# A state-space layer and attention in one kernel: a scan's end in seven PSUM banks, both norms from one formula, and the step size's chain inside the query and key products

## The chip, the cores and the metric

The kernel runs on one core of one Trainium2 chip. The metric is the time of one execution on the device in microseconds (us). The profile is that of one further execution. Engines: TensorE (PE; PEld is its weight load), VectorE (DVE), ScalarE (ACT), GpSimd (POOL) and SyncE (SP), which issues nearly all DMAs.

## What is computed

A gated block with two layers over four sequences of 512 rows of 512 values (`x`) and a context of 256 values per row. The first layer is a Mamba layer on the context, gated by the normed rows; the second is attention with rotary positions and a mixture of experts. Cut from the reference, with the names of the kernel's batches `s` (first layer) and `b` (second):

```python
x = einsum('ed,bld->bel', in_proj_w, hidden_states)          # in-projection
u = silu(conv(x, conv_w, 4 taps) + conv_b)
x_dbl = einsum('ke,bel->bkl', x_proj_w, u)                   # dt_lo, B, C
delta = softplus(einsum('er,brl->bel', dt_proj_w, dt_lo) + dt_proj_b)
def step(state, xs):
    d_t, B_t, C_t, u_t = xs
    dA = exp(d_t[..., None] * A)
    state = state * dA + (d_t * u_t)[..., None] * B_t[:, None, :]
    return (state, einsum('bn,ben->be', C_t, state))
y = (scan(step) + D * u) * silu(z)                           # z: the layer-normed rows of x
```

The attention that follows norms the new rows twice: a layer norm, (x - m) / sqrt(v + 1e-5), and on its result an RMS norm with 1e-6 under the root. Then come queries, keys (both rotated), values, a causal softmax in 16 heads of 32, an output product, another RMS norm, a router with top 2 of 8 experts, and a shared expert.

## The kernel before

**Rounds.** `round_(b, s)` runs for b from -1 to 3 with s = b + 1: the attention of batch b beside the Mamba scan of batch s. I call a round by its b. Each engine has its own program, with the same order of rounds; semaphores tie them. A round has a projection stage and then 16 units (`units(b, s)`, 64 scans of 128x512, 16 quads of heads). Round -1 has no attention (s = 0 alone), and round 3 no scan (`last_units`). After it comes the expert stage (`moe_stage`), which the change doesn't touch.

**A scan's end.** A scan (L1616, VectorE) of step k needs its decay (`decay`, L1174, ScalarE, exp into a PSUM bank) and its input (`driven`, L2095, GpSimd, `DU` times a row of B in one of four slots of `GB`). TensorE turns four states at a time (`turn_states`, L652) and VectorE adds them, weighted, to `YA` (`add_state`, L1626). For s > 0 all states go through one bank, `HT0`, so that each group waits for the addition before; for s = 0 two banks take turns. After the last addition TensorE turns the gate z (`turn_z`, L663, 16 transposes, two banks), VectorE multiplies (`scan_out`, L1633) and adds the result to the rows in `xa` (x1, L1637).

**The projection stage.** VectorE takes the statistics of x1; GpSimd makes both norms' factors in ten operations on 128x4 (`norms`, L2112 to L2121), each behind the one before; ScalarE scales the rows (`rows`, L1188), TensorE turns them, ScalarE and VectorE split them in a high and a low part (`h1_round`, `h1_rest`), TensorE makes the values. Between these lie the next batch's in-projection (L602), its convolution (ScalarE `conv_start`, VectorE `conv`) and what is left of the batch before: `finish(b - 1, 3, step)`, the last 128 rows' output product, norm and router.

**The products.** The loop over m from 0 to 7 then makes four query and four key products (`product`, 12 matmuls each), ScalarE adds a bias (`bias`, L1201), TensorE rotates (`rotate`, L696), GpSimd multiplies by the cosine (`rope_cos`, L2127) and VectorE by the sine and adds (`rope_out`, L1658 and L1662). Beside these, for m from 2 to 5, one quarter each of the step size delta: product (`delta`, L642), absolute value on ScalarE, relu on VectorE. Its softplus ends behind the loop: exp for m = 6, then Ln (`delta_log`, another table of ScalarE), and on VectorE four times `delta_sum` (L1598) and `delta_u` (L1604). The first `driven` waits for all four sums, because `GB` and the softplus' tile `TS` are one piece of memory.

The eight PSUM banks are `A[0]` to `A[3]` (together `SB`, named scores in traces), bank4 (`CX`, `WK`), bank5 (`PB`), and bank6 and bank7 (`HT0`, `HT1`). The lines that set the scan's end:

```python
def state_bank(s, q):
    return (HT0, A[0])[q % 2] if s == 0 else HT0
def decay_bank(s, k):
    return (HT1, A[1])[k % 2] if s == 0 else HT1
```

## Time and profile before

| | us |
|---|---|
| median of 3 runs | 1853.08 |
| lowest and highest | 1849.81, 1853.17 |
| the profiled execution, whole | 1852.96 |
| its span, first to last instruction | 1851.2 |
| busy: PE, DVE, ACT, POOL | 1504.1, 1180.0, 892.6, 806.3 |
| mean granted clock of TensorE, share of full speed | 0.878 |

The profiled execution is 0.1 us from the median, so that its timeline can be read against the median without a correction; 1.8 us of it lie outside the span. TensorE has the largest share (81%), but a sum over the span says little, since its stages have different limits. Round 0 begins at about 187 us, round 1 at 436, round 2 at 690 and round 3 at 945, each with its projection stage (90 to 95 us with a scan to follow); the expert stage fills the time from about 1165 us on. TensorE's clock has two levels, 1.2 and 2.4 GHz; 1.00 in a row is the upper one, 0.50 the lower.

### The profile page before, as it was taken

The page shows a single profiled execution, that of the slowest core. Times are in us where ns is not written, and L with a number is a line of the kernel's source. Part 1 is how long each engine was busy: PE and PEld are TensorE (multiplying, and loading weights), DVE is VectorE, ACT ScalarE, POOL GpSimd, SP SyncE. Part 2 cuts the span into 40 slices and gives each one's busy share as a digit, 9 for nine tenths or more (in the row PEclk, how much of TensorE's full clock was granted, in tenths as well). Part 3 has the DMA queues.
Part 4 walks back from the last instruction along what each step waited for, and adds up shares of the span by engine and source line. Part 5 has one row for each costly group of instructions (what it writes and reads, how often), then busy time and mean ns, then how long its engine had stood idle before and what let it go on. Part 6 is the DMA issues. An engine that isn't in the chain of part 4 may idle for free.

```text
span 1851.2 us, 26612 instructions
## 1 busy us (share of the span) xinstructions
PE 1504.1 (81%) x9104; PEld 1157.0 (63%) x9104; DVE 1180.0 (64%) x1731; ACT 892.6 (48%) x1974; POOL 806.3 (44%) x809
## 2 busy tenths in 40 slices
PE   5246787777967778877869798979999999999994
PEld 2134454555645555545547566768787899999973
DVE  4689758997579986599964443343333566665545
ACT  3443246775356763567742565111122666666510
POOL 0587026663156541366533221124332455555544
PEclk8555896988967898978889899989999999999997
DMA  5620001111101211002103210932220777777464
GB/s 184 260 76 29 1 24 29 59 57 34 42 18 39 72 41 33 9 29 58 47 28 113 100 36 24 352 103 80 80 86 1 285 248 268 236 258 248 168 215 162
DMA packets 94485, 195.74 MB, mean 106 GB/s; under 512 B 8768, under 2 KB 25664, under 8 KB 91024
## 3 DMA queue, kind: packets, MB, share of 16 engines
q1 hardware_dynamic: 89232, 177.26, 28.0%
q0 software_dynamic: 5120, 16.78, 2.7%
q8 instruction: 74, 1.21, 0.3%
q14 instruction: 59, 0.48, 0.1%
HBM read 140.40 MB, written 53.61 MB: 105 GB/s over the span
## 4 chain that ended last, share of the span: by engine, by line
PE 41%; issue 6%; DVE 6%; POOL 3%; ACT 2%; DMA 0%; DVEq 0%; SPq 0%; ACTq 0%; POOLq 0%
PE scores L588 20%; PE bank L588 11%; PE bank L770 2%; POOL yab L2279 2%; PE bank L720 2%; DVE YA L1626 1%; PE bank L652 1%; DVE HS L1616 1%; PE scores L707 1%; PE bank L735 1%; PE bank L997 1%; POOL lal L2272 1%; ACT bank L1174 0%; DVE nm L1668 0%; PE scores L710 0%
## 5 line engine op out<-in xcount | busy, mean ns | idle before, releaser
L2095 POOL TENSOR_TENSOR GB<-DU,BB 128x512 f32<-128x512 f32 x256 | 325.7, 1293 | 70.0 <-DVE DL L1598 46.0
L652 PE MATMUL bank<-ident,HS 128*128 128x128 f32 x896 | 183.0, 339 | 171.8 <-DVE YA L1626 115.7
L1616 DVE TENSOR_TENSOR_SCAN HS<-bank,GB 128x512 f32<-128x512 f32 x224 | 272.9, 1218 | 41.2 <-ACT bank L1174 16.3
L652 PEld LDWEIGHTS bank<-ident,HS 128*128 128x128 f32 x896 | 124.7, 171 | 217.3 <-DVE YA L1626 145.8
L1174 ACT ACTIVATE bank<-DL,aneg 128x512 f32<-128x512 f32 x224 | 154.8, 691 | 133.9 <-DVE HS L1616 133.0
L1626 DVE SCALAR_TENSOR_TENSOR YA<-bank,Ct,YA 128x512 f32<-128x512 f32 x224 | 165.9, 740 | 20.1 <-PE bank L652 18.0
L720 PE MATMUL bank<-ident,EX 128*128 128x128 f32 x640 | 131.4, 306 | 41.5 <-ACT PT L1217 23.4
L588 PE MATMUL scores<-xth,wgh 128*128 128x256 f32 x552 | 158.0, 286 | 2.1 <-DVE fa L1977 1.2
L588 PE MATMUL scores<-xth,wgl 128*128 128x256 f32 x552 | 156.1, 283 | 0.0
L588 PE MATMUL scores<-xtl,wgh 128*128 128x256 f32 x552 | 156.0, 283 | 0.0
L1209 ACT ACTIVATE EX<-scores,nm 128x128 f32<-128x128 f32 (+3 forms) x256 | 132.1, 520 | 33.0 <-DVE nm L1668 31.9
L1217 ACT ACTIVATE PT<-bank 128x128 f32<-128x128 f32 (+3 forms) x256 | 110.1, 430 | 65.8 <-PE bank L720 58.3
L720 PEld LDWEIGHTS bank<-ident,EX 128*128 128x128 f32 x640 | 79.6, 153 | 81.0 <-issue 50.2
L2234 POOL TENSOR_TENSOR wgl<-wgr,wgh 128x768 fp32r<-128x768 f32 x54 | 110.9, 2057 | 30.3 <-ACT wgh L1426 30.3
L2251 POOL TENSOR_TENSOR fal<-fa,fah 128x512 fp32r<-128x512 f32 x30 | 38.7, 1290 | 164.8 <-ACT fah L1455 164.6
L588 PEld LDWEIGHTS scores<-xth,wgh 128*128 128x128 f32 x552 | 105.6, 191 | 3.7 <-DVE fa L1977 1.6
L588 PE MATMUL scores<-hah,wgh 128*128 128x512 f32 x272 | 106.6, 392 | 1.4 <-issue 1.4
L588 PE MATMUL scores<-hal,wgh 128*128 128x512 f32 x272 | 106.3, 391 | 0.0
L588 PE MATMUL scores<-hah,wgl 128*128 128x512 f32 x272 | 106.3, 391 | 0.0
L588 PEld LDWEIGHTS scores<-xtl,wgh 128*128 128x128 f32 x552 | 105.7, 191 | 0.9
L2138 POOL TENSOR_TENSOR ctl<-cn,cth 128x128 fp32r<-128x128 f32 x64 | 29.3, 458 | 176.0 <-ACT cth L1228 175.9
L588 PEld LDWEIGHTS scores<-xth,wgl 128*128 128x128 f32 x552 | 105.6, 191 | 0.0
(272 smaller groups left out, 3731.4 us busy)
## 6 DMA issues: line engine op xcount, KB each, us to landing
wgr<-wffn_in SPq DMA_DIRECT2D x108, 384.0 KB, 6.5
wdr<-wffn_in SPq DMA_DIRECT2D x81, 256.0 KB, 2.9
BB<-b_scratch SPq DMA_DIRECT2D x64, 256.0 KB, 3.2
xg<-V SPq DMA_DIRECT2D x1, 11776.0 KB, 40.4
xr<-xg SPq DMA_DIRECT2D x23, 512.0 KB, 5.8
yg<-ysb SPq DMA_DIRECT2D x23, 512.0 KB, 6.5
hah<-hhd SPq DMA_DIRECT2D x5, 1024.0 KB, 13.4
hal<-hhd SPq DMA_DIRECT2D x5, 1024.0 KB, 15.1
```

Of the source, the lines that this page charges most:

```text
L588: mm = nc.tensor.matmul(out_, parts[a](k), rhs_parts[b](k), start=(k == 0 and j == 0), stop=(k == n - 1 and j == 2))
L652: mm = nc.tensor.transpose(state_bank(s, q)[:, et * P:(et + 1) * P], HS[:, n % 2, et, tt * P:(tt + 1) * P], ident[:])
L720: mm = nc.tensor.transpose(turned_bank(b, v)[:, kb * P:(kb + 1) * P], EX[:, a, kb * P:(kb + 1) * P], ident[:])
L770: mm = nc.tensor.matmul(into, parts[a](k), rhs_parts[c](k), start=(k == 0 and j == 0), stop=(k == n - 1 and j == 2))
L1174: nc.scalar.activation(decay_bank(s, k), DL[:, et, :], ACT.Exp, scale=aneg[:, et, n:n + 1]).then_inc(dA_ready, 1)
L1209: nc.scalar.activation(EX[:, a, 0:W], SB[:, a, 0:W], ACT.Exp, bias=nm[:, a:a + 1], accum_out=rs[:, q % 2, a:a + 1]).then_inc(ex_done, 1)
L1217: nc.scalar.activation(PT[:, a, 0:W], turned_bank(b, v)[:, 0:W], ACT.Copy).then_inc(pt_done, 1)
L1616: nc.vector.tensor_tensor_scan(HS[:, n % 2, et, :], decay_bank(s, k), GB[:, k % 4, :], 0.0, ALU.mult, ALU.add).then_inc(scan_done, 1)
L1626: nc.vector.scalar_tensor_tensor(YA[:, tt, :], state_bank(s, q), Ct[:, tt, n:n + 1], YA[:, tt, :], ALU.mult, ALU.add).then_inc(y_acc, 1)
L2095: nc.gpsimd.tensor_tensor(GB[:, k % 4, :], DU[:, et, :], BB[:, n % 2, :], ALU.mult).then_inc(gb_ready, 1)
L2234: nc.gpsimd.tensor_tensor(wgl[raw][:, c, :], wgr[raw][:, c * 2 * EW:(c + 1) * 2 * EW], wgh[raw][:, c, :].bitcast(f32), ALU.subtract).then_ ...
L2251: nc.gpsimd.tensor_tensor(fal[:, b % 2, c, :], fa[:, s % 2, :], fah[:, b % 2, c, :].bitcast(f32), ALU.subtract).then_inc(f_al, 1)
```

## The change

1. **A scan's end.** The last three groups of states go to A[0], A[2] and A[3] instead of `HT0`; the four groups of z go to bank5, A[1], A[0] and A[2] (`z_bank`). With bank6 these are seven banks for the eight groups (A[0] and A[2] twice). The waits follow: `turn_z` waits for an addition only where it takes a bank again, and the next batch's first in-projection for the fourth last addition instead of a gate product.
2. **Norms.** With v the variance and m the mean, the product of both norms' factors is (v (1 + 1e-6) + 1e-11) ** -0.5. It is made first, in five operations, for which `rows` waits; the layer norm's own factors, which only the residual needs, follow in four. Nine instead of ten.
3. **The last rows of the batch before.** Their square sum (`finish` step 1 on ScalarE) comes after `rows`, their rescaling (step 2) after `h1_round`, and TensorE's transposes after the first value product, where they came sooner.
4. **The step size.** All four `delta` products are made for m = 2 and 3, two each. Exp follows for m = 4, the four Ln for m = 5, three sums on VectorE for m = 4 and the fourth for m = 5, the first input (`driven`) and the first decay for m = 6.
5. **The start of the units.** VectorE scans once before the first row maximum and again directly after it; ScalarE makes the second decay before the exponentials, GpSimd two inputs ahead. The first scores wait for the last rotation's sine part (`rope_s`), and each of the first four quads for its own key.

The diff, cut to its core:

```diff
         def state_bank(s, q):
+            if q >= NB - 3:
+                return (A[0], A[2], A[3])[q - (NB - 3)]
             return (HT0, A[0])[q % 2] if s == 0 else HT0
+
+        def z_bank(tt):
+            return (PB, A[1], A[0], A[2])[tt]
...
-                if et < 2:
-                    at(pe, y_z, T4 * s - 1 + et)
-                else:
+                if et == 0:
+                    at(pe, y_acc, NB * s - 3)
+                if et >= 2:
                     pe.wait_ge(cv_tap, 12 * s + 3 * (et - 1))
...
-                if q > (s == 0):
+                if q == NB - 3 and s == 0:
+                    pe.wait_ge(y_acc, NB - 4)
+                if (s == 0) < q < NB - 3:
                     at(pe, y_acc, NB * s + q - (s == 0))
...
-                if tt < 2:
-                    pe.wait_ge(y_acc, NB * s + NB)
-                else:
-                    pe.wait_ge(y_z, T4 * s + tt - 1)
+                if tt >= 2:
+                    pe.wait_ge(y_acc, NB * s + NB + tt - T4)
                 for rt in range(T4):
-                    mm = nc.tensor.transpose(HT[tt % 2][:, rt * P:(rt + 1) * P],
+                    mm = nc.tensor.transpose(z_bank(tt)[:, rt * P:(rt + 1) * P],
...
                 if q == 0:
                     pe.wait_ge(v_done, T4 * b + T4)
-                    pe.wait_ge(qk_done, 8 * b + 8)
+                    pe.wait_ge(rope_s, 8 * b + 8)
+                if q < T4:
+                    pe.wait_ge(qk_done, 8 * b + T4 + q + 1)
...
-                        if 2 <= m < 6:
-                            delta(s, m - 2)
+                        if 2 <= m < 4:
+                            delta(s, 2 * m - 4)
+                            delta(s, 2 * m - 3)
...
             def rows(b, tt):
                 if tt == 0:
-                    act.wait_ge(a_norm, 10 * b + 10)
+                    act.wait_ge(a_norm, 9 * b + 5)
...
             def probs(b, v):
+                if v == 0:
+                    act.wait_ge(qk_done, 8 * b + 8)
...
             def finish(b, i, step):
                 if step == 0:
+                    act.wait_ge(a_norm, 9 * b + 9)
...
             def units(b, s):
+                decay(s, 1)
...
-                    if scn and 2 <= m < 6:
-                        delta_relu(s, m - 2)
+                    if scn and 1 <= m < 3:
+                        delta_relu(s, 2 * m - 2)
+                        delta_relu(s, 2 * m - 1)
+                    if scn and m == 4:
+                        for et in range(3):
+                            delta_sum(s, et)
+                            delta_u(s, et)
+                    if scn and m == 5:
+                        delta_sum(s, 3)
+                        delta_u(s, 3)
...
+                norm(1, nc.gpsimd.tensor_tensor(a[:, 5, :], var, onee[:], ALU.mult))
+                norm(2, nc.gpsimd.tensor_tensor(a[:, 7, :], a[:, 5, :], epsp[:], ALU.add))
+                norm(3, nc.gpsimd.tensor_tensor(a[:, 8, :], a[:, 7, :], mhalf[:], ALU.pow))
+                norm(4, nc.gpsimd.tensor_tensor(a[:, 6, :], mean, a[:, 8, :], ALU.mult))
+                norm(5, nc.gpsimd.tensor_tensor(a[:, 9, :], a[:, 6, :], mone[:], ALU.mult))
...
+                        if scn and m == 6:
+                            driven(s, 0)
```

**TensorE at the end of s = 1's scan**, before (HS are states, ZS the gate rows; the words in brackets name semaphores: y_added the additions, y_gated the gate products, z_done the gate rows):

```order
L652 MATMUL bank6<-ident,HS 128x128 [waits y_added,scan_done]
L652 MATMUL bank6<-ident,HS 128x128 x3
L652 MATMUL bank6<-ident,HS 128x128 [waits y_added]
L652 MATMUL bank6<-ident,HS 128x128 x3
L652 MATMUL bank6<-ident,HS 128x128 [waits y_added]
L652 MATMUL bank6<-ident,HS 128x128 x3
L652 MATMUL bank6<-ident,HS 128x128 [waits y_added]
L652 MATMUL bank6<-ident,HS 128x128 x3
L663 MATMUL bank6<-ident,ZS 128x128 [waits y_added,z_done]
L663 MATMUL bank6<-ident,ZS 128x128 x3
L663 MATMUL bank7<-ident,ZS 128x128 [waits y_added,z_done]
L663 MATMUL bank7<-ident,ZS 128x128 x3
```

and in the changed kernel:

```order
L662 MATMUL bank6<-ident,HS 128x128 [waits y_added,scan_done]
L662 MATMUL bank6<-ident,HS 128x128 x3
L662 MATMUL scores<-ident,HS 128x128 x12
L671 MATMUL bank5<-ident,ZS 128x128 [waits z_done]
L671 MATMUL bank5<-ident,ZS 128x128 x3
L671 MATMUL scores<-ident,ZS 128x128 [waits z_done]
L671 MATMUL scores<-ident,ZS 128x128 x3
L671 MATMUL scores<-ident,ZS 128x128 [waits y_added,z_done]
L671 MATMUL scores<-ident,ZS 128x128 x3
L671 MATMUL scores<-ident,ZS 128x128 [waits y_added,z_done]
L671 MATMUL scores<-ident,ZS 128x128 x3
```

The three later state groups follow the first as one row of twelve transposes with no wait, and the first two gate groups with none but that for the gate rows.

**ScalarE at the end of round 1's products**, before (EX<-bank,bqk is a bias, GB<-GB first the exp and then the Ln, bank<-DL,aneg a decay, EX,rs<-scores,nm an exponential of the softmax, PT a transposed copy):

```order
L1201 ACTIVATE EX<-bank,bqk 128x512 [waits rope_cos,qk_rotated,qk_product]
L1160 ACTIVATE GB<-GB 128x2048 [waits delta_abs]
L1201 ACTIVATE EX<-bank,bqk 128x512 [waits rope_cos,qk_rotated,qk_product]
L1164 ACT_TABLE_LOAD
L1164 ACTIVATE GB<-GB 128x512 [waits delta_exp] x4
L1174 ACT_TABLE_LOAD [waits delta_done]
L1174 ACTIVATE bank<-DL,aneg 128x512 [waits delta_relu]
L1209 ACTIVATE EX,rs<-scores,nm 128x128 [waits probs_transposed,row_max] x4
L1217 ACTIVATE PT<-bank 128x128 [waits pv_ready,probs_transposed]
L1174 ACTIVATE bank<-DL,aneg 128x512 [waits scan_done,delta_done]
```

and in the changed kernel:

```order
L1212 ACTIVATE EX<-bank,bqk 128x512 [waits rope_cos,qk_rotated,qk_product]
L1171 ACTIVATE GB<-GB 128x2048 [waits delta_abs]
L1212 ACTIVATE EX<-bank,bqk 128x512 [waits rope_cos,qk_rotated,qk_product]
L1175 ACT_TABLE_LOAD
L1175 ACTIVATE GB<-GB 128x512 [waits delta_exp] x4
L1212 ACTIVATE EX<-bank,bqk 128x512 [waits rope_cos,qk_rotated,qk_product]
L1185 ACT_TABLE_LOAD [waits delta_done]
L1185 ACTIVATE bank<-DL,aneg 128x512 [waits delta_relu]
L1212 ACTIVATE EX<-bank,bqk 128x512 [waits rope_cos,qk_rotated,qk_product]
L1185 ACTIVATE bank<-DL,aneg 128x512 [waits scan_done,delta_done]
L1222 ACTIVATE EX,rs<-scores,nm 128x128 [waits probs_transposed,row_max,qk_ready]
L1222 ACTIVATE EX,rs<-scores,nm 128x128 [waits probs_transposed,row_max] x3
```

Exp, Ln and both table loads stand one to three biases sooner, a bias stands between the Ln and the table load of the decay, and two decays stand ahead of the exponentials, where there was one.

**VectorE at the same place**, before (EX<-scores,rope and QK are a rotation, DL<-DL,GB and DU a pair of sums, TENSOR_REDUCE the row maximum, HS a scan):

```order
L1598 TENSOR_TENSOR DL<-DL,GB 128x512 [waits delta_relu,delta_log]
L1604 SCALAR_TENSOR_TENSOR DU<-DU,DL 128x512 [waits xdbl_product,du_term_product,delta_done]
L1598 TENSOR_TENSOR DL<-DL,GB 128x512 [waits delta_relu,delta_log]
L1604 SCALAR_TENSOR_TENSOR DU<-DU,DL 128x512 [waits xdbl_product,du_term_product,delta_done]
L1668 TENSOR_REDUCE nm<-scores 128x4 [waits scores_ready]
L1616 SCALAR_TENSOR_TENSOR HS<-bank,GB 128x512 [waits input_ready,decay_ready,v_product,qk_product]
L1673 RECIPROCAL ri<-rs 128x4 [waits inverse_widened,exp_ready]
L1616 SCALAR_TENSOR_TENSOR HS<-bank,GB 128x512 [waits decay_ready,input_ready]
L1668 TENSOR_REDUCE nm<-scores 128x4 [waits scores_ready]
```

and in the changed kernel:

```order
L1616 TENSOR_TENSOR DL<-DL,GB 128x512 [waits delta_relu,delta_log]
L1622 SCALAR_TENSOR_TENSOR DU<-DU,DL 128x512 [waits xdbl_product,du_term_product,delta_done]
L1676 SCALAR_TENSOR_TENSOR EX<-scores,rope 128x512 [waits qk_ready,qk_rotated]
L1680 SCALAR_TENSOR_TENSOR QK<-PT,EX 128x512 [waits rope_cos,rope_sin]
L1616 TENSOR_TENSOR DL<-DL,GB 128x512 [waits delta_relu,delta_log]
L1622 SCALAR_TENSOR_TENSOR DU<-DU,DL 128x512 [waits xdbl_product,du_term_product,delta_done]
L1676 SCALAR_TENSOR_TENSOR EX<-scores,rope 128x512 [waits qk_ready,qk_rotated]
L1680 SCALAR_TENSOR_TENSOR QK<-PT,EX 128x512 [waits rope_cos,rope_sin]
L1676 SCALAR_TENSOR_TENSOR EX<-scores,rope 128x512 [waits qk_ready,qk_rotated]
L1680 SCALAR_TENSOR_TENSOR QK<-PT,EX 128x512 [waits rope_cos,rope_sin]
L1634 SCALAR_TENSOR_TENSOR HS<-bank,GB 128x512 [waits input_ready,decay_ready,v_product,qk_product]
L1686 TENSOR_REDUCE nm<-scores 128x4 [waits scores_ready]
```

The last pair of sums stands between the sixth and the seventh rotation, three pairs ahead of the sixth, and the first scan follows the eighth rotation, ahead of the row maximum.

## Rows read from the trace of the kernel before

**Rows 1.** Windows: PE, PEld, DVE, ACT, POOL busy (count), PEclk, DMA share, GB/s

```profile
437.00:443.00 6.00, 2.25 (x14) 1.51 (x14) 3.00 (x4) 0.94 (x2) 0.46 (x1) 0.94 0.00 0
443.00:451.00 8.00, 7.91 (x30) 6.35 (x30) 6.22 (x10) 0.00 (x0) 0.00 (x0) 0.62 0.00 0
492.00:522.00 30.00, 30.00 (x115) 18.86 (x113) 14.26 (x18) 11.78 (x16) 9.03 (x8) 1.00 0.00 1
522.00:530.00 8.00, 1.36 (x13) 0.89 (x12) 7.79 (x12) 4.30 (x7) 1.46 (x2) 0.64 0.00 0
530.00:700.00 170.00, 127.88 (x1033) 90.16 (x1034) 152.99 (x191) 115.46 (x303) 98.16 (x108) 0.81 0.15 46
1250.00:1850.00 600.00, 565.64 (x3332) 501.98 (x3331) 300.46 (x493) 246.59 (x488) 284.56 (x235) 0.98 0.53 180
```

**Rows 2.** Timeline, VectorE, round 1's start: start, duration, what, [idle before <-releaser]

```profile
437.17 0.75 DVE L1626 SCALAR_TENSOR_TENSOR YA<-bank,Ct,YA 128x512 f32<-128x512 f32 x1 [0.28 <-PE bank L652]
...
441.88 0.75 DVE L1626 SCALAR_TENSOR_TENSOR YA<-bank,Ct,YA 128x512 f32<-128x512 f32 x1 [0.82 <-PE bank L652]
...
447.46 2.73 DVE L1637 SCALAR_TENSOR_TENSOR xa<-YA,tg,xa 128x512 f32<-128x512 f32 x4
```

**Rows 3.** Timeline, TensorE, the same place

```profile
436.43 0.63 PE L652 MATMUL bank<-ident,HS 128*128 128x128 f32 x4 [0.20 <-DVE YA L1626]
```

**Rows 4.** Timeline, VectorE, end of round 1's products and first units

```profile
517.40 0.69 DVE L1658 SCALAR_TENSOR_TENSOR EX<-scores,rope 128x512 f32<-128x512 f32 x1 [2.47 <-PE scores L696]
...
523.97 0.69 DVE L1598 TENSOR_TENSOR DL<-DL,GB 128x512 f32<-128x512 f32 x1
...
528.67 0.69 DVE L1604 SCALAR_TENSOR_TENSOR DU<-DU,DL 128x512 f32<-128x512 f32 x1
...
530.69 1.22 DVE L1616 TENSOR_TENSOR_SCAN HS<-bank,GB 128x512 f32<-128x512 f32 x1 [0.72 <-POOL GB L2095]
...
534.91 1.22 DVE L1616 TENSOR_TENSOR_SCAN HS<-bank,GB 128x512 f32<-128x512 f32 x1 [0.30 <-ACT bank L1174]
```

**Rows 5.** Timeline, round 0's start: TensorE, VectorE, ScalarE

```profile
189.42 1.11 PE L652 MATMUL bank<-ident,HS 128*128 128x128 f32 x4
...
197.43 2.73 DVE L1637 SCALAR_TENSOR_TENSOR xa<-YA,tg,xa 128x512 f32<-128x512 f32 x4
...
205.54 0.78 ACT L1114 ACTIVATE GB<-bank,chan 128x512 f32<-128x512 f32 x1 [0.94 <-PE bank L602]
...
207.51 3.09 ACT L1188 ACTIVATE PT<-xa,ast 128x512 f32<-128x512 f32 x4 [1.19 <-POOL ast L2121]
```

**Rows 6.** Timeline, round 1's norms: GpSimd, ScalarE

```profile
453.08 0.20 POOL L2112 TENSOR_TENSOR ast<-amv,eps 128x4 f32<-128x4 f32 x1 [15.30 <-DVE amv L1563]
453.36 1.01 POOL L2113 TENSOR_TENSOR ast<-ast,mhalf 128x4 f32<-128x4 f32 x1
...
457.44 3.31 ACT L1188 ACTIVATE PT<-xa,ast 128x512 f32<-128x512 f32 x4 [0.57 <-POOL ast L2121]
```

**Rows 7.** Timeline, round 1's products: TensorE, ScalarE

```profile
501.80 1.02 PE L696 MATMUL scores<-EX,perm 128*128 128x512 f32 x2
502.75 1.12 PE L642 MATMUL bank<-xd,dtproj 16*128 16x512 f32 x2
...
520.85 1.28 ACT L1164 ACT_TABLE_LOAD   x1
522.14 2.19 ACT L1164 ACTIVATE GB<-GB 128x512 f32<-128x512 f32 x4
```

**Rows 8.** Chain that ended last, one product of round 3: start, duration, what

```profile
998.76 2.75 PE bank L588 x12
```

**Rows 9.** Line L1688 over the run: duration ns min/median/max, first and last start

```profile
L1688 DVE SCALAR_TENSOR_TENSOR xa<-XL,tg,xa x16: 750/752/1218, 320.8 to 1156.6; 128x512 f32<-128x512 f32 x16
```

**Rows 10.** Timeline, round 3: VectorE's last rotation, TensorE's first scores

```profile
1022.33 0.69 DVE L1662 SCALAR_TENSOR_TENSOR QK<-PT,EX 128x512 f32<-128x512 f32 x1
...
1023.13 0.81 PE L707 MATMUL scores<-QK 32*128 32x128 f32 x8 [5.28 <-issue]
```

74 lines of the change are left out of this document (37 added, 37 removed).

## The prediction

> **What bounds the kernel now.** I read the stages first, then the timelines of the engines between two scans. The kernel runs five rounds, and four times it passes from the end of one batch's scan over norms, values and query and key products to the next scan. Between these passages VectorE sets the pace: over 170 us of scan and attention it is busy 152.99 us [rows 1]. Inside them it isn't: from 492 to 522 us TensorE is busy all 30.00 us at full clock, while VectorE has 14.26. From 522 to 530 us TensorE has 1.36 us and VectorE 7.79, so there VectorE is the chain [rows 1]. Nothing loads or stores in those stretches (DMA share 0.00), so a passage is a chain of small steps. Whatever shortens it moves all later work forward, unless another engine is late next. The last 600 us, the expert layers, are TensorE's (565.64 us busy) and have no line of the change in them: they only start earlier.
>
> **Part 1, the scan's end.** In round 1 (times of that round, unless another is named) the four last state additions start every 1.57 us (437.17 to 441.88, three steps in 4.71) [rows 2], though one takes 0.75. Each waits for transposes into one bank, and these wait for the addition before [rows 3]. Then the 16 gate transposes share two banks with the four products on them, and x1 begins at 447.46 [rows 2]. With banks of their own the transposes stop waiting: TensorE has four every 0.43 us at full clock (it starts at 436.43 and four take 0.63 with the last one's tail of 0.2 [rows 3]), and VectorE becomes the chain. Its operations follow each other every 0.66 us here (the eight step-size operations: 523.97 to 528.67 is seven steps in 4.70, 0.67 each [rows 4]). Four additions from 437.17 end at 439.8, four gate products at 0.60 to 0.67 end at 442.3, so x1 begins **5.2 us earlier**. The first in-projection no longer waits for gate products, so TensorE goes on with the output product, behind nothing.
>
> Round 0 is different. There TensorE runs at the lower clock: four transposes take 1.11 us instead of 0.63 [rows 3, 5], so 0.85 to 0.91 from group to group. The third of the last four state groups stands at 189.42, so the first at 187.4 or so; the eighth group from there ends at 194.6 and the last gate product at 195.2, against 197.43 now [rows 5]: 2.2 us. This is half the gain, because two banks already alternated in this scan.
>
> **Part 2, the norms.** The ten operations on GpSimd start at 453.08, and ScalarE's normed rows, which wait for the tenth, at 457.44: 4.36 us [rows 6]. An ordinary one costs 0.28 from start to start (453.08 to 453.36), a power 1.01 and 0.08 of gap. The first five of the new order are four ordinary ones and one power: 3 x 0.28 + 1.09 + 0.20 = 2.1 us. The other four (1.9 us) run on behind, under ScalarE's 3.31 us of rows, and the residual that needs them comes a unit later. **2.25 us earlier**. ScalarE has something new in that place: the square sum of the last row (0.7 us) stood ahead of the rows, in the wait for GpSimd, and now stands behind them, while the rescaling (0.6 us) leaves the stretch between rows and rounding. I take 0.3 us back for this and the order of the tanh. The output product and the first in-projections must be done before the norms are. Behind the gate transposes the output product can start at 440.5 (436.43, eight groups of 0.43, a short wait for the third addition). If the two take as long as now, some 9 us to the end of ScalarE's second convolution start, they end at 449.5, and the norms at 450.1: close, but free. Rounds 1 and 2: 5.2 + 2.25 - 0.3 = **7.1 us each**. Round 3 has no convolution: 5.2 + 2.25 = 7.45.
>
> In round 0 the gain is cut. ScalarE starts its second convolution at 205.54 and the rows at 207.51 [rows 5]. 2.2 us earlier the second start is 203.3, ending at 203.95, while the norms end at 203.05. So the rows wait for TensorE's in-projection and start at 204.0: **3.5 us** instead of 4.5.
>
> **Part 3, the step size.** The delta products are moved, not saved: 1.05 us each (a pair of matmuls, 1.12 with its tail; the rotation ahead of it stands 0.95 sooner, at 501.80 [rows 7]) between the same eight products. They delay the fourth and fifth product by 1.05 and give it back before the seventh. Exp, Ln and the table loads move under products that take 2.75 us [rows 8]; ScalarE's biases are needed only one product later, and the worst slot (table load 1.28 and four Ln 2.19 [rows 7]) delays one bias by 0.4 us, which the next product covers. What leaves the end is VectorE's eight operations, 523.97 to 529.3, and what follows: the scan at 530.69 waited for GpSimd's first input and the third scan starts at 534.91 [rows 4]. These operations now stand between the rotations, 5.3 us of VectorE time. Laid out on the rows: VectorE starts the sixth rotation at 517.40 after 2.47 us idle [rows 4]; TensorE will be ready with it at 517.0, and with the fifth one product and one rotation sooner (2.75 + 0.95 [rows 7, 8]), at 513.4. That ends on VectorE at 515.0, three pairs of sums at 519.1, the sixth rotation at 520.6, the last pair at 521.9, the seventh and eighth at 524.8, where they ended at 524.0. The scan starts right there, its input ready since 522.6. The second scan waits for a decay behind it (2.0 us), the row maximum lies between, and the third waits for four exponentials, the second scores, a transposed copy and a decay: 524.8 + 6.0 = 530.8, against 534.91, **4.1 us**. Not the 5.9 by which the first scan moves: the exponentials now wait behind the first scan instead of ahead of it.
>
> From this comes a cost that the old trace shows only elsewhere. GpSimd's multiplications (1.29 us) now run beside VectorE operations with two inputs in SBUF. The residual sum, such an operation, has 0.75 us as its median and 1.22 as its longest [rows 9]. At 0.3 to 0.47 for two or three meetings I take off 0.8 us (bounds 0 and 1.9, four meetings at 0.47): **3.3 us** in rounds 0, 1 and 2. The rule of the Trainium skill (SBUF — State Buffer, Who interferes with whom) goes further: one of the two holds the shared port pair for its whole instruction and the other is blocked. By that rule four meetings would cost up to 4 x 1.29 = 5.2 us, and part 3 would be worth nothing; the rows' longest case is 0.47 us over the median, so I go by the rows.
>
> **Part 4, scores.** The first scores wait for the last rotation's first half instead of its whole. In round 3 that operation starts at 1022.33 and the scores at 1023.13 [rows 10]: **0.7 us** once. In the other rounds the scan is the chain. The new waits (ScalarE's exponentials for the last key, the residual for the ninth norm) are met long before.
>
> **The sum.** Round 0: 3.5 + 3.3 = 6.8. Rounds 1 and 2: 2 x (7.1 + 3.3) = 20.8. Round 3: 7.45 + 0.7 = 8.15. Together 35.8 us. The profiled execution took 1852.96 us (span 1851.2), the median is 1853.08, 0.1 us apart. 1853.0 - 35.8 = **1817 us**.
>
> **Rivals.**
> **A, the port.** Part 3 yields nothing, because GpSimd's early inputs and VectorE's sums block each other, and the rotations behind them come late. Three times 3.3 us are missing: 1853 - 25.9 = 1827. This is also what the rule above would give. For it: VectorE has 7.79 of 8 us busy at the end of the products, and work is added just ahead. Against: 0.47 us as the worst meeting [rows 9]. Chance 0.15.
> **B, the lower clock reaches further.** Rounds 1 and 2 behave like round 0, with rows that wait for the in-projection: 3.6 us less each, 1824. For it: the clock was 0.62 from 443 to 451 us [rows 1], which is just where output product and in-projection lie. Against: that fall came after TensorE had 2.25 us of work in 6, from 437 to 443, and those gaps go. Chance 0.12.
> **C, the clock stays up.** With the gaps gone, round 0 gets 7.1 instead of 3.5 and the port costs nothing (3 x 0.8): 1853 - 41.8 = 1811. The Trainium skill (TensorE: Matmul & The Clock Gate, What's actually happening) says that low clock is the default and activity lifts it. By that rule, the trace agrees: 0.62 after the idle stretch. But round 0's scan keeps TensorE at the lower clock throughout, so I give it 0.12.
> **D, slower.** The earlier hand-over breaks the clock of the projections. The products of a round take 30.00 us at clock 1.00 [rows 1]; at the lower of the two levels they would take 60. Four times 30 us more, less 35.8: 1937. It decides from 9 us of full-speed product work per round that runs at the lower level. For it: nothing but that the order ahead of the products changes. Against: even after a fall the clock was back at 1.00 from 492. Chance 0.03.
> **E, it doesn't come through**: each passage's gain is taken up by the wait for the last row's residual or by the scans' later start, leaving within 3.7 us of 1853. That needs 32 us of new waits for which I see no place. Chance 0.03.
>
> **How the numbers follow.** The forecast has 0.55, the rivals 0.15, 0.12, 0.12, 0.03 and 0.03. The range takes in A, B and C with their edges: 1809 to 1828. A measurement of this kernel tells about 0.2% (3.7 us) from no change. Faster by more: forecast, A, B and C, 0.94. Within: 0.03. Slower: 0.03.
>
> **What would show it.** Right: the last four additions 0.7 to 0.9 us apart and the gate products directly behind; x1 to stats some 5 us sooner in rounds 1 to 3; normed rows 2.1 us after GpSimd's first norm; the first scan less than 1 us behind the last rotation, the third some 6 us after the first. Wrong: if the rows of rounds 1 and 2 wait for a convolution start (B), if VectorE's sums or rotations last 1 us and more beside GpSimd (A), or if the third scan comes 8 us and more after the first. The unit stages must keep their lengths (170 us, 163 us); if they change, something that I haven't costed is at work.

## The result and the profile after

| kernel | median, us | range, us | ratio to before, 95% interval |
|---|---|---|---|
| before | 1851.71 (4 runs) | 1849.81 to 1853.17 | 1 |
| changed | 1825.62 (4 runs) | 1824.79 to 1826.48 | 0.9858 [0.9846, 0.987] |

The profiled execution of the changed kernel has a span of 1823.3 us against 1851.2, so 27.9 us went, where the sum of the prediction had 35.8. The time lies within the range, 8.6 us above the forecast and 1.4 below rival A. The stages show that the sum has one large error, in part 3. (The parts are those of the prediction: 1 the scan's end, 2 the norms, 3 the step size with the new start of the units, 4 the first scores.)

| gain, us (before less after) | round 0 | 1 | 2 | 3 |
|---|---|---|---|---|
| last scan to x1 | 3.26 | 5.25 | 5.26 | 5.27 |
| x1 to normed rows | 1.06 | 2.21 | 2.20 | 2.20 |
| normed rows to last rotation | -2.42 | -5.20 | -5.02 | -1.23 |
| last rotation to third scan | 4.82 | 4.82 | 4.82 | |
| third scan to last scan | -1.10 | -0.22 | 3.07 | |
| last rotation to first scores | | | | 0.73 |

The rest of round 3 and the expert layers gave back 1.8 us. These numbers are differences of start times (for the last rotation, its end) in the timelines of the two profiled executions. The unit stages (third to last scan) run the same instructions in both kernels and yet differ by up to 3 us between rounds and kernels, so a single profile can't carry a difference of 1 or 2 us there. The stretch from round 3's first scores to the end varies more: 825.2 to 830.0 us in the changed kernel and in the variants made from it, none of which changes anything there.

**The scan's end, as forecast.** VectorE's timeline at round 1's start, after (columns as in [rows 2]):

```profile
431.65 0.75 DVE L1644 SCALAR_TENSOR_TENSOR YA<-bank,Ct,YA 128x512 f32<-128x512 f32 x1 [0.27 <-PE bank L662]
432.32 2.06 DVE L1644 SCALAR_TENSOR_TENSOR YA<-scores,Ct,YA 128x512 f32<-128x512 f32 x3
434.29 0.68 DVE L1651 TENSOR_TENSOR YA<-bank,YA 128x512 f32<-128x512 f32 x1
434.89 1.87 DVE L1651 TENSOR_TENSOR YA<-scores,YA 128x512 f32<-128x512 f32 x3
436.69 2.73 DVE L1655 SCALAR_TENSOR_TENSOR xa<-YA,tg,xa 128x512 f32<-128x512 f32 x4
```

In [rows 2] the last four additions came every 1.57 us, each behind a wait for TensorE. Now four additions and four gate products follow each other without a gap, 5.04 us from the first to x1. The same place on TensorE's clock, by windows (columns as in [rows 1]):

```profile
437.00:443.00 6.00, 3.80 (x10) 1.50 (x8) 5.92 (x15) 1.55 (x2) 0.55 (x3) 1.00 0.00 0
443.00:445.00 2.00, 0.00 (x0) 0.00 (x0) 1.97 (x3) 0.55 (x1) 1.69 (x5) 0.65 0.00 0
445.00:452.00 7.00, 6.54 (x22) 4.49 (x23) 4.46 (x8) 6.40 (x12) 2.11 (x6) 0.61 0.10 37
```

```profile
437.20 3.60 PE L610 MATMUL bank<-cT,w_in 128*128 128x512 f32 x8
445.41 3.96 PE L681 MATMUL scores<-ident,PT 128*128 128x128 f32 x16 [4.61 <-ACT PT L1199]
```

The output product (L596, ahead of these rows) and the first half of the in-projection (L610) run at clock 1.00 and are done by 440.8. TensorE then has nothing to do for 4.61 us, until the normed rows come, and the clock is down when it transposes them. The fall of [rows 1] has moved behind them; it hasn't gone.

**The norms, as forecast.** These are GpSimd and then ScalarE, round 1, after:

```profile
442.29 0.20 POOL L2139 TENSOR_TENSOR ast<-amv,onee 128x4 f32<-128x4 f32 x1 [10.03 <-DVE amv L1581]
...
444.22 0.20 POOL L2143 TENSOR_TENSOR ast<-ast,mone 128x4 f32<-128x4 f32 x1
```

```profile
444.45 1.52 ACT L1199 ACTIVATE PT<-xa,ast 128x512 f32<-128x512 f32 x2 [2.84 <-POOL ast L2143]
```

From the first norm to the first row it is 2.16 us, 4.36 in [rows 6].

**The products' end, not as forecast.** VectorE, round 1, after; it is busy from 503.84 to 513.97 without a gap:

```profile
503.84 0.69 DVE L1616 TENSOR_TENSOR DL<-DL,GB 128x512 f32<-128x512 f32 x1
...
506.51 1.78 DVE L1616 TENSOR_TENSOR DL<-DL,GB 128x512 f32<-128x512 f32 x1
508.33 0.69 DVE L1622 SCALAR_TENSOR_TENSOR DU<-DU,DL 128x512 f32<-128x512 f32 x1
508.94 0.68 DVE L1676 SCALAR_TENSOR_TENSOR EX<-scores,rope 128x512 f32<-128x512 f32 x1
...
512.31 1.06 DVE L1680 SCALAR_TENSOR_TENSOR QK<-PT,EX 128x512 f32<-128x512 f32 x1
513.29 0.68 DVE L1676 SCALAR_TENSOR_TENSOR EX<-scores,rope 128x512 f32<-128x512 f32 x1
514.60 1.67 DVE L1680 SCALAR_TENSOR_TENSOR QK<-PT,EX 128x512 f32<-128x512 f32 x1 [0.63 <-POOL PT L2153]
516.19 1.21 DVE L1634 TENSOR_TENSOR_SCAN HS<-bank,GB 128x512 f32<-128x512 f32 x1
...
522.31 1.22 DVE L1634 TENSOR_TENSOR_SCAN HS<-bank,GB 128x512 f32<-128x512 f32 x1 [0.48 <-ACT bank L1185]
```

GpSimd beside it:

```profile
501.94 1.29 POOL L2153 TENSOR_TENSOR PT<-EX,rope 128x512 f32<-128x512 f32 x1 [2.31 <-ACT EX L1212]
506.02 1.72 POOL L2153 TENSOR_TENSOR PT<-EX,rope 128x512 f32<-128x512 f32 x1 [2.79 <-ACT EX L1212]
511.02 1.79 POOL L2121 TENSOR_TENSOR GB<-DU,BB 128x512 f32<-128x512 f32 x1 [3.28 <-DVE DL L1616]
512.78 1.71 POOL L2153 TENSOR_TENSOR PT<-EX,rope 128x512 f32<-128x512 f32 x1
```

The third sum (506.51) met a cosine product (506.02): 1.78 us instead of 0.69, and GpSimd 1.72 instead of 1.29. All such meetings in these traces follow one pattern. A sum, an update or a second half that starts while one of GpSimd's 128x512 products runs ends 0.55 us after that product does (after the second, where it meets two), so it loses what is left of the product less 0.14 us: the third sum met its last 1.23 us. GpSimd is held up in the same way: its product of 506.02 started inside the update before that sum, and such products end 1.12 to 1.20 us after VectorE's operation. Operations with an input in PSUM (the first halves of the rotations, 508.94 and 513.29) kept 0.68 beside the same GpSimd work. The last second half waited 0.63 us for a cosine product that stood behind the first scan input in GpSimd's queue, and then took 1.67, because it met the second scan input.

**A fall of the clock that was not foreseen.** TensorE, round 1, after:

```profile
485.27 1.98 PE L650 MATMUL bank<-xd,dtproj 16*128 16x512 f32 x4
487.18 0.50 PE L596 MATMUL bank<-h1h,wah 128*128 128x512 f32 x1
...
489.22 0.63 PE L596 MATMUL bank<-h1h,wah 128*128 128x512 f32 x1
```

```profile
487.00:491.00 4.00, 4.00 (x12) 3.06 (x12) 1.50 (x2) 0.80 (x2) 0.00 (x0) 0.62 0.00 0
```

Behind the four 16-row matmuls of two delta products the granted clock went to the lower level, and eight of the next product's twelve matmuls came every 0.43 us instead of 0.23: 1.6 us. Round 2 shows the same (733.5 to 736.9), round 0 doesn't, and behind the second four (492.56) it doesn't happen either. TensorE was busy all the time, so no idle share would have warned of it.

### The profile page after: what moved, and what is told of

The parts are those of the page before. It is cut to its first block, busy times and chain, and to the rows that moved or that the text cites. A ratio compares the mean times of both kernels' runs of the same rounds, so it can differ in the third digit from the quotient of the medians.

```text
span 1823.3 us, 26633 instructions
## 1 busy us (share of the span) xinstructions
PE 1495.2 (82%) x9104; PEld 1155.2 (63%) x9104; DVE 1183.9 (65%) x1731; ACT 891.7 (49%) x1974; POOL 810.3 (44%) x807
## 4 chain that ended last, share of the span: by engine, by line
PE 54%; DVE 17%; issue 17%; ACT 6%; POOL 5%; DMA 1%; DVEq 0%; SPq 0%; ACTq 0%; POOLq 0%
PE scores L596 21%; PE bank L596 14%; DVE HS L1634 6%; DVE YA L1644 5%; PE bank L662 3%; PE bank L730 3%; PE bank L780 2%; ACT bank L1185 2%; PE scores L717 2%; PE bank L745 2%; POOL yab L2309 2%; PE scores L704 1%; PE bank L1008 1%; PE bank L650 1%; POOL GB L2121 1%
## 5 line engine op out<-in xcount | busy, mean ns | idle before, releaser
L662 PE MATMUL bank<-ident,HS 128*128 128x128 f32 x856 | 175.9, 341 | 161.2 <-DVE YA L1644 105.9
L662 PEld LDWEIGHTS bank<-ident,HS 128*128 128x128 f32 x856 | 120.4, 172 | 202.9 <-DVE YA L1644 132.9
L1644 DVE SCALAR_TENSOR_TENSOR YA<-bank,Ct,YA 128x512 f32<-128x512 f32 x214 | 157.5, 736 | 10.6 <-PE bank L662 9.0
L596 PE MATMUL scores<-xth,wgh 128*128 128x256 f32 x552 | 158.2, 287 | 2.2 <-DVE fa L2003 1.3
L596 PE MATMUL scores<-xth,wgl 128*128 128x256 f32 x552 | 156.3, 283 | 0.0
L596 PE MATMUL scores<-xtl,wgh 128*128 128x256 f32 x552 | 156.2, 283 | 0.0
L596 PEld LDWEIGHTS scores<-xth,wgh 128*128 128x128 f32 x552 | 105.7, 191 | 3.8 <-DVE fa L2003 1.7
L596 PE MATMUL scores<-hah,wgh 128*128 128x512 f32 x272 | 106.7, 392 | 1.4 <-issue 1.4
L596 PE MATMUL scores<-hal,wgh 128*128 128x512 f32 x272 | 106.4, 391 | 0.0
L596 PE MATMUL scores<-hah,wgl 128*128 128x512 f32 x272 | 106.4, 391 | 0.0
L596 PEld LDWEIGHTS scores<-xtl,wgh 128*128 128x128 f32 x552 | 105.8, 192 | 0.9
L596 PEld LDWEIGHTS scores<-xth,wgl 128*128 128x128 f32 x552 | 105.7, 192 | 0.0
```

What stands on the lines that cost most here:

```text
L596: mm = nc.tensor.matmul(out_, parts[a](k), rhs_parts[b](k), start=(k == 0 and j == 0), stop=(k == n - 1 and j == 2))
L662: mm = nc.tensor.transpose(state_bank(s, q)[:, et * P:(et + 1) * P], HS[:, n % 2, et, tt * P:(tt + 1) * P], ident[:])
L1644: nc.vector.scalar_tensor_tensor(YA[:, tt, :], state_bank(s, q), Ct[:, tt, n:n + 1], YA[:, tt, :], ALU.mult, ALU.add).then_inc(y_acc, 1)
```

## The experiments

The theory after the result: parts 1, 2 and 4 gave nearly the whole gain, as costed. Part 3 gave nothing in rounds 1 and 2, because VectorE's moved sums and GpSimd's products hold each other up at SBUF (I call it the port), because the eighth cosine product stands behind a waiting input (queue), and because the clock falls behind the delta pairs (clock). Rivals: part 3 gave its gain and another part failed; the port costs nothing and VectorE was simply full.

**no_chain.** The changed kernel without part 3, that is without items 4 and 5 of the change except the earlier scores. On VectorE, for example:

```diff
-                    if scn and m == 4:
-                        for et in range(3):
-                            delta_sum(s, et)
-                            delta_u(s, et)
-                    if scn and m == 5:
-                        delta_sum(s, 3)
-                        delta_u(s, 3)
...
+                if scn:
+                    for et in range(T4):
+                        delta_sum(s, et)
+                        delta_u(s, et)
```

> The changed kernel without its third part: delta products one per product, Exp, Ln, sums and first scan input behind the query and key products, scans in the order of before; scan end, norms and scores as changed. Prediction's sum: part 3 is worth 3.3 us in each of three rounds, so this kernel is 9.9 us slower than the changed one, about 1835.5 us. What the trace of after says: part 3 gave 1.6 us in round 0 and nothing in rounds 1 and 2, so about 1827 us, and the stage from the last xd row to the third scan has the same length as in the changed kernel within 2 us in each round.

Measured: 1826.68 us, ratio 0.9859 [0.9833, 0.9885]. The changed kernel has 0.9858, so part 3 is worth nothing that the whole time shows; the interval is about 5 us to either side, and the sum's 9.9 lie outside it. From last scan to third scan round 1 takes 93.40 us here and 93.41 in the changed kernel, round 2 93.41 and 93.45, round 0 91.39 and 89.77. So 1.6 us is left of part 3, in round 0.

**part1_only.** The kernel before with seven banks at the scan's end, no more:

```diff
+            if q >= NB - 3:
+                return (A[0], A[2], A[3])[q - (NB - 3)]
             return (HT0, A[0])[q % 2] if s == 0 else HT0
+        def z_bank(tt):
+            return (PB, A[1], A[0], A[2])[tt]
```

> The kernel before with the first part alone: the last three state groups and the four gate groups of a scan in banks of their own, the first in-projection no longer behind the gate products. The prediction's term: 2.2 us in round 0 and 5.2 in rounds 1 to 3, 17.8 in all: 1836 beside 1853.9 of before. By the stage lengths of after (3.26, 5.25, 5.26, 5.27) it is 19.0: 1834.9. If the norms or the rows wait for something that the scan end used to cover, x1 to rows gets longer than 9.98 us and the time is 1840 or more.

Measured: 1834.60 us, ratio 0.9902 [0.9875, 0.9929]: 18.2 us of 1853, where the sum had 17.8. From x1 to the rows it stays at 9.98 in rounds 1 and 2. The step from here to no_chain (norms and scores) is 0.9902 - 0.9859, 8.0 us; the sum had 1.3 + 2 x 1.95 + 2.25 + 0.7 = 8.15. By the ratios these sums are settled only to about 5 us, the width of the intervals; the stages settle them more closely.

**split_pairs.** One delta product of each pair in the middle of a product:

```diff
+                    def middle(m=m):
+                        if scn and m == 2:
+                            turn_c(s)
+                            delta(s, 0)
+                        if scn and m == 3:
+                            delta(s, 2)
```

> The changed kernel, but the first delta product of each pair is issued in the middle of a query/key product instead of directly ahead of the second, so the pairs of 16-row matmuls never run back to back. Clock theory: in rounds 1 and 2 the granted clock fell to 0.50 for some 3.4 us behind the first double pair and eight of twelve matmuls took 0.43 us instead of 0.23 (8 x 0.20 = 1.6 us). Then the product stays at 0.23 us a matmul in all rounds and the kernel gains 2 x 1.6 = 3.2 us: 1822.4. Rival: the fall comes from the stage's timing and not from the pair, it stays somewhere near, and the time is 1825.6 within 1.

Measured: 1826.21 us, ratio 0.9852 [0.9836, 0.9869]. The clock did what was expected. TensorE, round 1, at the same place:

```profile
487.00 1.12 PE L650 MATMUL bank<-xd,dtproj 16*128 16x512 f32 x2
488.05 0.50 PE L596 MATMUL bank<-h1h,wah 128*128 128x512 f32 x1
...
489.07 0.39 PE L596 MATMUL bank<-h1l,wah 128*128 128x512 f32 x1
```

No matmul of rounds 1 and 2's query and key products is at 0.63 us any more. But the stage to the third scan became only 0.8 us shorter in rounds 1 and 2 and 0.75 longer in round 0: cutting the products costs about 0.8 us of its own. So the clock costs 1.6 us in each of two rounds, this cure gives half of it back there and costs 0.75 in the third, and the whole time is the same.

**input_last.** GpSimd makes the first scan input behind the eighth cosine product (`m == 7` in place of `m == 6`).

> The changed kernel, but GpSimd makes the first scan input behind the eighth cosine product instead of ahead of it. Queue theory: the eighth cosine product (512.78 in round 1) stood behind the first input, which waits for the fourth sum (510.94); moved ahead it runs at about 509.1, the eighth rotation's second half no longer waits 0.63 us and no longer meets GpSimd (1.67 us instead of 0.69), and the first scan starts 1.2 to 1.6 us earlier: 3 to 4.5 us in three rounds, 1821 to 1822.5. Rival: the first input, which cannot start before the fourth sum, is itself late next, and the gain is under 1 us in all.

Measured: 1824.33 us, ratio 0.9841 [0.9825, 0.9857]. The stage to the third scan is 0.3 to 0.5 us shorter, not 1.2 to 1.6. The wait went, the last second half took 1.04, but the cosine product now met the fourth update, which grew to 1.63:

```profile
509.75 0.69 DVE L1616 TENSOR_TENSOR DL<-DL,GB 128x512 f32<-128x512 f32 x1
510.47 1.63 DVE L1622 SCALAR_TENSOR_TENSOR DU<-DU,DL 128x512 f32<-128x512 f32 x1
...
514.41 1.04 DVE L1680 SCALAR_TENSOR_TENSOR QK<-PT,EX 128x512 f32<-128x512 f32 x1
```

The queue theory falls as a cause of its own: what the queue gave, the port took.

**thin_cosines.** GpSimd's last three cosine products of the rounds with a scan cover 8 of 512 columns. This kernel leaves out the rest of them, so it only prices what they cost VectorE.

```diff
+                w = L if m < 5 or b == B - 1 else 8
```

> The changed kernel, but GpSimd's last three cosine products of the rounds with a scan behind them cover 8 of 512 columns (the rest of the last three rotations is left as it was: this leaves work out). It prices what GpSimd's multiplications cost VectorE there. Port theory: in round 1 of after the third sum took 1.78 us instead of 0.69, the seventh rotation's second half 1.06 and the eighth's 1.67 instead of 0.69, behind a wait of 0.63: 3.1 us a round. Without partners they take 0.69 and the first scan starts 2.5 to 3.1 us earlier in each of three rounds: 1825.6 - 8.5 = 1817 (1816 to 1818). Rival: these operations would last as long anyway, or TensorE's last rotation (it waited 0.55 us for VectorE) is late next: 1823 or more.

Measured: 1820.12 us, ratio 0.9822 [0.9797, 0.9848]; the stage to the third scan is 2.2 us shorter in rounds 1 and 2 and 1.0 in round 0, where the way from the last scan to the rows took 1.2 us longer in this execution. VectorE's sums over the whole run, as groups by line (count | busy us, mean ns | idle before), of the changed kernel and of this one:

```profile
L1616 DVE TENSOR_TENSOR DL<-DL,GB 128x512 f32<-128x512 f32 x16 | 14.3, 892 | 3.3 <-ACT GB L1175 3.1
```

```profile
L1616 DVE TENSOR_TENSOR DL<-DL,GB 128x512 f32<-128x512 f32 x16 | 11.0, 688 | 4.3 <-ACT GB L1175 4.3
```

The 1.1 us per round on the third sum are GpSimd's doing, so the rival that VectorE was simply full falls. The last second halves still took 1.06 and 1.20 us, beside scan inputs, which is why 3.1 was not reached; the whole time, 1820.12, lies between the 1817 of the port and the 1823 of its rival.

**early_chain.** The split pairs, Exp and Ln one product sooner, sums behind the fourth and fifth rotation, the first decay and the first input for m = 5. The sums:

```diff
-                    if scn and m == 4:
-                        for et in range(3):
+                    if scn and 3 <= m < 5:
+                        for et in (2 * m - 6, 2 * m - 5):
                             delta_sum(s, et)
                             delta_u(s, et)
```

> The changed kernel with split pairs, and with Exp one product earlier, Ln one product earlier, the four sums behind the fourth and fifth rotation instead of the fifth and sixth, the first input behind the sixth cosine product. Theory: from 503.8 us on VectorE was the chain in round 1 (12.5 us of work without a gap of note), with 1.86 and 2.38 us idle just ahead. If sums move into that idle time the first scan starts about 4 us earlier in each of three rounds, besides the 3.2 us of the clock: 1825.6 - 15 = 1810. Port theory: wherever the sums stand they meet a cosine product and both take 1.7 us instead of 0.69 and 1.29, so each round still loses 1 to 2 us: 1812 to 1816. If VectorE is not the chain: 1822.

Measured: 1818.64 us, ratio 0.981 [0.9794, 0.9826]. The stage to the third scan is 3.4 us shorter in rounds 1 and 2 and 0.5 in round 0, where the way from the last scan to the rows took 1.3 us longer in this execution (it does in several of these kernels). The sums were not held up and took 0.68 or 0.69 each. VectorE is the chain in this stretch, and filling its idle time ahead of the sixth rotation pays, by half of what was expected: the second halves are still 1.07, 1.67 and 1.06 us.

**inputs_early.** early_chain with the first two scan inputs sooner on GpSimd, each behind its own sum instead of all four:

```diff
-                    pool.wait_ge(dl_s, T4 * s + T4)
...
-                        if scn and m == 5:
-                            driven(s, 0)
+                        if scn and 5 <= m < 7:
+                            driven(s, m - 5)
```

> early_chain (1818.6) with GpSimd's first two scan inputs each behind the sum that they read (not behind all four), the first behind the sixth cosine product, the second behind the seventh. Queue theory: the seventh cosine product no longer stands behind a waiting first input, so the seventh rotation's second half loses its wait of 0.35 us and its 1.67 us becomes about 1.06, and fewer inputs are left at the end: about 1 us a round, 1815.5. Port theory: every GpSimd operation that is moved meets another VectorE operation, and the sum of lengths stays: 1818.6 within 1.

Measured: 1826.49 us, ratio 0.9854 [0.9829, 0.988]: 8 us slower than early_chain and as slow as the changed kernel; 5.4 of them are in the three stages to the third scan. GpSimd, then VectorE, round 1:

```profile
504.84 1.74 POOL L2130 TENSOR_TENSOR GB<-DU,BB 128x512 f32<-128x512 f32 x1
506.54 1.75 POOL L2162 TENSOR_TENSOR PT<-EX,rope 128x512 f32<-128x512 f32 x1
508.24 1.74 POOL L2130 TENSOR_TENSOR GB<-DU,BB 128x512 f32<-128x512 f32 x1
```

```profile
505.35 1.78 DVE L1628 TENSOR_TENSOR DL<-DL,GB 128x512 f32<-128x512 f32 x1
507.17 1.67 DVE L1634 SCALAR_TENSOR_TENSOR DU<-DU,DL 128x512 f32<-128x512 f32 x1
508.76 1.76 DVE L1628 TENSOR_TENSOR DL<-DL,GB 128x512 f32<-128x512 f32 x1
```

The two engines take turns. Three VectorE operations last 5.2 us instead of 2.1. Neither expectation was right. Work put there early is not neutral, it cost 1.0 to 1.1 us for each of these VectorE operations, which met 1.12 to 1.23 us of GpSimd's.

**inputs_scan3.** inputs_early with the third scan ahead of the second row maximum.

> inputs_early with the third scan ahead of the second row maximum on VectorE, and its decay ahead of the second copied transpose on ScalarE. In after the third scan came 6.12 us after the first (4.23 before): VectorE waited 1.32 us for scores and 0.48 for the decay. If VectorE is the chain from there, the third scan comes 4.3 us after the first and the round is 1.2 to 1.8 us shorter: 4 to 5 us under inputs_early, 1811. Rival: the row maximum is 0.6 us later and with it the attention units, which set the pace as much; the stage from third to last scan gets longer by what was gained: no difference.

Measured: 1824.71 us, ratio 0.984 [0.9813, 0.9866]. The third scan comes 4.27 us after the first instead of 6.12, and the stage from it to the last scan is 155.49, 155.80 and 155.75 us against 153.65, 153.92 and 153.90: all of it is given back. The rival holds. Where the units' pace is set wasn't looked into; here an earlier third scan alone wasn't worth anything.

**rs_psum.** The first half of each rotation goes to PSUM:

```diff
-                nc.vector.scalar_tensor_tensor(RS[:, m % 2, :], A[m % 2][:], f, rope[:, 1, :],
+                nc.vector.scalar_tensor_tensor(A[2 + m % 2], A[m % 2][:], f, rope[:, 1, :],
...
-                nc.vector.scalar_tensor_tensor(QK[:, m, :], RC[:, m % 2, :], f, RS[:, m % 2, :],
+                nc.vector.scalar_tensor_tensor(QK[:, m, :], RC[:, m % 2, :], f, A[2 + m % 2],
```

> The changed kernel, but the first half of each rotation is written to a PSUM bank (those of the third and fourth value product) instead of SBUF, so VectorE's second half reads one operand from SBUF and one from PSUM; the first scores wait for the eighth rotation's end again. Port theory: only VectorE operations with two SBUF inputs are held up by GpSimd (in after the first halves, with one PSUM input, took 0.68 us beside GpSimd, the second halves 1.02 to 1.67). Then all second halves take 0.69 us, the wait of 0.63 before the last one shrinks, and the first scan starts 1.5 to 2 us earlier in each of three rounds: 1825.6 - 5 + 0.7 (scores of round 3) = 1821. Rival: the length comes from GpSimd's load as such, whichever memory is read, or PSUM writes cost as much: 1826.

Measured: 1823.39 us, ratio 0.9839 [0.9818, 0.986]. Groups by line over the whole run, the second halves of the changed kernel and of this one:

```profile
L1680 DVE SCALAR_TENSOR_TENSOR QK<-PT,EX 128x512 f32<-128x512 f32 x32 | 35.3, 1103 | 2.9 <-POOL PT L2153 1.9
```

```profile
L1682 DVE SCALAR_TENSOR_TENSOR QK<-PT,scores 128x512 f32<-128x512 f32 x32 | 22.0, 687 | 2.6 <-POOL PT L2155 1.6
```

From 1103 to 687 ns in the mean, with the same GpSimd work beside it: only operations with two SBUF inputs are held up. GpSimd is spared too: its product that starts inside one of these second halves takes 1.26 us instead of 1.71. The last rotation ends 1.45 to 1.5 us sooner in each round with a scan, of which 0.4 to 0.5 go back, since the scores now wait for it and the third scan for them. By the medians the kernel is 2 to 3.5 us faster than the changed one, about the width of its interval, so the time per operation is shown and the gain of the whole only likely.

**finish_order.** TensorE transposes the old batch's last row ahead of the first value product again.

> The changed kernel, but TensorE transposes the last row of the batch before (the second step of its finish) ahead of the first value product again. In round 3 the stage from the rounding to the last rotation was 53.12 us against 51.89 before: the four transposes (0.6 us) left an idle stretch of 3.6 us and stand between products, and 9 instead of 7 value matmuls ran at the lower clock (0.43 us). If this is the cause, that stage goes back to 51.9 and the time to 1824.4. Rival: ScalarE's order of the same steps is the cause: 1825.6, stage 53.1.

Measured: 1822.29 us, ratio 0.9832 [0.9813, 0.9852]. In round 3 the stage from the rounding to the last rotation went from 53.12 to 52.48, half of the 1.2 us; the transposes are back in TensorE's idle time, but they now wait for ScalarE, whose order of these steps was left:

```profile
946.42 1.09 PE L761 MATMUL bank<-ident,hp 128*128 128x128 f32 x4 [3.21 <-ACT hp L1255]
947.16 0.78 PE L596 MATMUL scores<-wah,h1h 128*128 128x512 f32 x1
```

This doesn't show that the order of these steps cost the 1.2 us. part1_only has the old order on both engines and takes 52.66 us in this stage, 0.8 more than before. What differs is the clock in the first value product: 7 matmuls took 0.63 us or more in the kernel before, 11 in part1_only, 9 in the changed kernel, 8 in this one, each 0.2 us above the others. In the changed kernel's 1.2 us some 0.4 are two more of these matmuls; the rest is the transposes between the products and what waits behind them. Why the number of slow matmuls differs is open, and the kernels with the changed kernel's order here and the rotations as they were range from 52.87 to 54.05. The median fell by 3.3 us; that the edit is the cause of this isn't shown, since this stage gave 0.6 and the spread of the rest of the program is larger.

Round 0, which this edit doesn't touch, took 3.6 us longer here than in the changed kernel. 1.6 of them are the fall of the clock behind the delta pairs, which this execution has in round 0 too:

```profile
242.34 1.98 PE L650 MATMUL bank<-xd,dtproj 16*128 16x512 f32 x4
...
245.09 0.63 PE L596 MATMUL bank<-h1h,wal 128*128 128x512 f32 x1
```

From the normed rows to the third scan round 0 takes 74.25 us here, 74.25 in no_chain and 72.65 in the changed kernel. So what part 3 kept in round 0 is there only when the clock doesn't fall.

**early_psum.** early_chain with the edits of rs_psum and finish_order.

> early_chain (1818.6) with both edits of this call: rotations' first halves in PSUM, last row's transposes ahead of the values. Port theory: the second halves of the sixth to eighth rotation (1.07, 1.67, 1.06 us) take 0.69 and the wait of 0.35 goes, about 1.9 us in each of three rounds; less 1.2 in round 3 for the transposes, plus 0.7 for the scores: 1812.5. Rival: TensorE's last products become the chain and leave half of it: 1815.

Measured: 1808.95 us (1805.26 to 1813.45), ratio 0.9756 [0.9734, 0.9777]. It is the fastest here, 0.9 to 1.0% below the changed kernel. VectorE, round 1:

```profile
505.66 0.69 DVE L1693 SCALAR_TENSOR_TENSOR QK<-PT,scores 128x512 f32<-128x512 f32 x1
507.30 0.70 DVE L1689 SCALAR_TENSOR_TENSOR scores<-scores,rope 128x512 f32<-128x512 f32 x1 [0.95 <-PE scores L705]
508.03 0.69 DVE L1693 SCALAR_TENSOR_TENSOR QK<-PT,scores 128x512 f32<-128x512 f32 x1
508.64 0.69 DVE L1689 SCALAR_TENSOR_TENSOR scores<-scores,rope 128x512 f32<-128x512 f32 x1
509.37 0.69 DVE L1693 SCALAR_TENSOR_TENSOR QK<-PT,scores 128x512 f32<-128x512 f32 x1
509.97 1.22 DVE L1645 TENSOR_TENSOR_SCAN HS<-bank,GB 128x512 f32<-128x512 f32 x1
```

From last scan to third scan round 1 takes 88.65 us: 4.8 less than in the changed kernel, 11.8 less than before. VectorE now waits 0.95 us for TensorE, which is late next. Together the edits gave 9.7 us on top of early_chain, more than the 6.1 of the expectation; its profiled span is only 5.6 us below that of early_chain, so part of the 9.7 is the spread between executions.

## Why the prediction was right, and where it was not

**Part 1: right.** 17.8 us summed, 18.2 measured by itself. 5.2 a round was 5.25 to 5.27 in rounds 1 to 3. That VectorE becomes the chain, with an operation every 0.66 us, holds line by line. Round 0 gained 3.3 instead of 2.2, because the lower clock that I took for it didn't last: the last twelve gate transposes took 1.47 us, against 2.32 in finish_order, where it gained 2.4. In the other kernels with this scan end it gained up to 3.4.

**Part 2: right for the norms.** 2.25 us was 2.20 to 2.21, and in round 0 the rows did wait for the second convolution start: 1.06 instead of the 1.3 taken, and 0 to 0.2 in six of the ten other kernels with this part, those with the slower scan end in round 0. The 0.3 taken off for ScalarE's order doesn't stand: from the rows to the last rotation no_chain lost 0.4 and 0.2 us in rounds 1 and 2 against before, but part1_only, with the old order, lost the same (67.03 us in both rounds, no_chain 67.00). It comes with the earlier scan end, a cost that the sum didn't have. In round 3 the same stretch lost 1.2 us where the sum had nothing; 0.8 of it is in part1_only too, by the clock in the value product (finish_order), and only the rest may belong to the moved steps.

**Part 3: wrong, 9.9 us summed, 1.6 by the stages and about 0 by the medians.** The layout of round 1, set beside the trace by distance from ScalarE's copy of x_dbl (`xd`, 483.00 before, 470.43 after), shows the steps. VectorE's fifth rotation was to start 30.4 us after it (513.4 less 483.0) and started 31.6 after: "they delay the fourth and fifth product by 1.05" counted the moved matmuls but not that they run back to back, and the clock took 1.2 more. The third sum took 1.1 us more, the seventh's and eighth's second halves 0.4 and 1.0, with 0.6 of waiting: 3.1 us of port and queue against the 0.8 taken off. 1.2 + 3.1 - 0.8 = 3.5 us, and the term was 3.3. Round 0 had no fall of the clock in this execution and kept 1.6.

The failed step is the price of a meeting, and beside it the delta pairs, whose effect on the clock the sum put at nothing. I took 0.3 to 0.47 us from [rows 9] and two or three meetings; the runs show that a meeting costs what is left of GpSimd's operation less 0.14 us, 1.0 to 1.1 us for the third sum and the last second half. Line L1688 gave a mild value because its maximum only shows the meetings that happened to occur: its 1.22 us met the last 0.67 us of a scan input, and in part1_only the same line reached 1.84, beside two inputs. It was also wrong that the old trace shows the cost only elsewhere. It stood in the second halves of the rotations, in the kernel before, which rs_psum shows to be meetings too: most take 0.99 to 1.03 us, and one in each of rounds 1 to 3 takes 1.5. GpSimd and VectorE, before, round 1:

```profile
492.60 1.28 POOL L2127 TENSOR_TENSOR PT<-EX,rope 128x512 f32<-128x512 f32 x1 [0.28 <-ACT EX L1201]
```

```profile
492.91 1.51 DVE L1662 SCALAR_TENSOR_TENSOR QK<-PT,EX 128x512 f32<-128x512 f32 x1
```

**Part 4: right**, 0.73 against 0.7.

**The rivals.** A came true by its amount: with part 3 at nothing it gave 1827, and 1825.6 was measured. Of the 3.5 us lost in rounds 1 and 2 the port and the queue made two thirds, the clock one third. The rule of the Trainium skill that the prediction set against [rows 9] (SBUF — State Buffer, Who interferes with whom) names a VectorE operation with two SBUF inputs against a GpSimd operation that reads SBUF, one holding the pair and the other blocked. The traces agree on who is blocked (1.78 us for two SBUF inputs, 0.68 with one in PSUM), and inputs_early shows its price; GpSimd's operation, when it starts second, is the one that waits (1.72 instead of 1.29). Weighing the row above the rule was the mistake. The rule's four whole meetings, 5.2 us, were too many all the same: the port and the queue took 3.1. B did not occur in rounds 1 and 2, where the norms and not the in-projection released the rows. C is half right: the clock stayed at 1.00 through the output product and the first half of the in-projection, but it fell in the 4.6 us that TensorE now waits behind them, and the port cost more, not nothing. D's loss appeared in miniature: the clock does break inside the products, for 1.6 us and not for 30, but behind the delta pairs (split_pairs) and not from the earlier hand-over. E did not occur.

Why the total was near nonetheless: 35.8 - 9.9 = 25.9 us for the parts that worked, and the runs give 26.1 by the medians. Two smaller errors nearly cancel: round 0's scan end gave 1.1 us more than summed, round 3 about 1.2 less. The range held because it reached to A, not because part 3 was understood.
